# Moving the first attention pass ahead of the scan's preparation, with a new timetable for the scans

## The reference

```python
# first attention: 16 heads in 8 pairs, 4 sequences of 256 tokens, slots M=64
q, k, v, s = x@Wq, x@Wk, x@Wv, clip(x@Ws)      # per head
# slot attention in closed form: e = exp(s), z = cumsum(e) over time
ok = tril(q k^T) @ e / z ; p = softmax(ok * scale) ; o = tril((p/z) e^T) @ v
o = rmsnorm(o) * g_norm_weight * silu(x@Wg) ; x = layernorm(x + o@Wo)
# state-space block: u = silu(conv(in_proj @ ctx)); dt, B, C = x_proj @ u
delta = softplus(dt_proj @ dt + bias)           # 256 channels
for n in range(16):                             # state index
    state_n[t] = state_n[t-1] * exp(delta*A_n) + (delta*u) * B_n[t]
    y += state_n * C_n
```

## Time and profile before

| | us |
|---|---|
| time, median of 3 runs | 1022.68 (1022.05 to 1022.96) |
| profiled execution, its own time | 1022.48 |
| its span | 1020.7 |
| PE busy | 884.8 (87%) |
| DVE busy | 766.3 (75%) |
| ACT busy | 503.4 (49%) |
| POOL busy | 423.3 (41%) |

### The profile page before, as it was taken

How to read it: one execution, slowest core, us unless ns; L and a number is a source line. 1 busy time by engine, 2 the same in 40 slices (tenths; PEclk the granted TensorE clock), 3 DMA queues, 4 the chain that set the end, 5 groups by cost and what they waited for, 6 DMA issues and landing times.

```text
span 1020.7 us, 16012 instructions
## 1 busy us (share of the span) xinstructions
PE 884.8 (87%) x5239; PEld 571.3 (56%) x5239; DVE 766.3 (75%) x1372; ACT 503.4 (49%) x971; POOL 423.3 (41%) x338
## 2 busy tenths in 40 slices
PE   6789999999999999977788999899826785899886
PEld 2446565656666666655576766677614573343443
DVE  6759797878787878879783554666467688998797
ACT  3554545444444445444344433345523338898485
POOL 1244738292837464554204433243277332121013
PEclk9789999999999999997899999999957898999998
DMA  5812112112121121100805999899643100000001
GB/s 183 277 60 67 62 57 68 61 51 77 51 64 64 62 67 62 62 1 1 248 22 181 303 301 298 271 288 285 187 126 93 51 1 2 6 7 7 1 6 37
DMA packets 53840, 105.08 MB, mean 103 GB/s; under 512 B 8569, under 2 KB 26305, under 8 KB 53281
## 3 DMA queue, kind: packets, MB, share of 16 engines
q1 hardware_dynamic: 48033, 88.76, 26.7%
q0 software_dynamic: 5760, 15.74, 6.0%
HBM read 87.34 MB, written 17.14 MB: 102 GB/s over the span
## 4 chain that ended last, share of the span: by engine, by line
PE 44%; DVE 27%; DMA 9%; issue 8%; POOL 5%; ACT 5%; SPq 2%; DVEq 0%; POOLq 0%; ACTq 0%
PE ps L717 5%; PE ps L893 4%; PE ps L802 4%; DMA w_dn<-in_w_dn 4%; PE ps L682 4%; PE ps L905 3%; DVE row_max L2550 3%; POOL key_part L1453 3%; PE ps L1225 2%; PE ps L672 2%; DVE state L2009 2%; DMA key_part<-y_dram,slot_idx 2%; DMA y_dram<-y_out 2%; PE ps L730 2%; PE ps L1211 2%
## 5 line engine op out<-in xcount | busy, mean ns | idle before, releaser
L1374 POOL TENSOR_TENSOR state<-state,c_row 128x1024 f32<-128x1024 f32 x32 | 77.3, 2416 | 181.7 <-DVE state L2009 99.1
L1425 POOL DMA_INDIRECT xg<-x_dram,tok_of x68 | 65.4, 962 | 147.3 <-PE ps L951 102.1
L717 PE MATMUL ps<-w_vg,xT 128*128 128x512 f32 x256 | 118.9, 609 | 7.6 <-DVE th L2033 7.6
L893 PE MATMUL ps<-w_gv,xgT 128*128 128x352 f32 (+1 forms) x272 | 91.2, 480 | 0.5 <-DMA w_dn<-in_w_dn 0.2
L1367 POOL TENSOR_TENSOR drive<-du,b_row 128x1024 f32<-128x1024 f32 x32 | 90.3, 2823 | 0.2
L672 PE MATMUL ps<-xT,w_qks 128*128 128x512 f32 x192 | 85.0, 593 | 0.7 <-DMA w_qks<-in_wqks 0.7
L2020 DVE TENSOR_TENSOR aT<-ps,tri 128x768 f32<-128x768 f32 x64 | 60.0, 956 | 33.8 <-PE ps L682 33.3
L2009 DVE TENSOR_TENSOR_SCAN state<-decay,drive 128x1024 f32<-128x1024 f32 x32 | 83.9, 2624 | 0.0
L2550 DVE TENSOR_REDUCE row_max<-ps 128x4 f32<-128x1024 f32 x64 | 74.3, 1218 | 7.1 <-PE ps L1190 6.3
L717 PEld LDWEIGHTS ps<-w_vg,xT 128*128 128x128 f32 x256 | 47.4, 196 | 56.7 <-issue 45.6
L1377 POOL TENSOR_TENSOR y<-y,state 128x1024 f32<-128x1024 f32 x32 | 75.4, 2357 | 2.5
(11 more groups left out here) (308 smaller groups left out, 1981.2 us busy)
## 6 DMA issues: line engine op xcount, KB each, us to landing
w_gv<-in_w_gv SPq DMA_DIRECT2D x68, 352.0 KB
w_dn<-in_w_dn SPq DMA_DIRECT2D x68, 176.0 KB
y_dram<-y_out SPq DMA_DIRECT2D x68, 128.0 KB, 7.0
b_row<-x_dbl_dram SPq DMA_DIRECT2D x16, 512.0 KB, 3.5
c_row<-x_dbl_dram SPq DMA_DIRECT2D x16, 512.0 KB, 4.8
y_dram<-blank SPq DMA_DIRECT2D x4, 1408.0 KB, 13.1
w_vg<-in_wvg SPq DMA_DIRECT2D x8, 512.0 KB, 3.2
w_qks<-in_wqks SPq DMA_DIRECT2D x8, 384.0 KB, 2.9
```

What stands on the lines that cost most here:

```text
L717: last = mm(bank(PJ + t % 2), xT[:, k, t * P:(t + 1) * P], w_vg[:, k, :], start=(k == 0), stop=(k == KD - 1))
L893: last = mm(ps[:, j, 0:2 * F], x_of(k), w(k), start=(k == 0), stop=(k == KD - 1))
L1374: G.tensor_tensor(state[:, n % 2], state[:, n % 2], c_row[:, j], ALU.mult).then_inc(read_out, 1)
```

## The change

Pass 0 of the attention is placed ahead of the scan's preparation. `conv` now lies in `state`, `aux` and `aux2` in `drive` (four buffers in place of two), `x_pad` in the rows' buffers, `x_dbl` in `wT`. The projections for `x_dbl` (`inner_rows`) and for the step size (`step_size`) are PE work inside pass 0, in the banks of the scores; the softplus is spread over pass 0 on ACT and DVE. No unit of the scan runs in pass 0, five run in each of passes 1 to 6, two in the last. Two of the five follow each other behind the masks; the first stands ahead of the gates. The drives are made four units ahead. POOL reads the two units behind the masks only when both are scanned. The slot sums and their product with epsilon lie in PSUM from pass 1 on. The loops over passes are unrolled.

```diff
+SLOTS = ("front", "masks", "masks2", "gated", "clip")
+SCANS = ((),) + (SLOTS,) * 6 + (("front", "gated"),)
+        drive = sb("drive", [P, LEADS, TOK])
+        conv = state[:]
+        x_dbl = wT[0:XD]
+        aux = drive[:, 0:ET]
+        aux2 = drive[:, ET:2 * ET]
...
                 project_vg(0)
+                if i == 0:
+                    scores(0, range(2, 3))
                 project_vg(1)
+                if i == 0:
+                    scores(0, range(3, 4))
+                    inner_rows()
...
                 project_vg(2)
+                if i == 0:
+                    step_size(0)
                 project_vg(3)
...
+                    if i == 0 and t == 4:
+                        step_size(1)
...
+            def read_and_drive(i, slots):
+
+                units = [SCAN_AT[i, slot] for slot in slots if slot in SCANS[i]]
+                for m in units:
+                    read_of(m, units[-1] if "masks2" in slots else m)
+                for m in units:
+                    if m + LEADS < STATE_UNITS:
+                        drive_of(m + LEADS)
...
+            for i in range(PAIRS):
+                read_and_drive(i, ("front",))
+                read_and_drive(i, ("masks", "masks2"))
+                if i < PAIRS - 1:
+                    pool.wait_ge(zT_ready, i + 2)
+                read_and_drive(i, ("gated", "clip"))
...
+            def exp_plus_one():
+                dve.wait_ge(scan_act, 13)
+                V.tensor_scalar(aux, conv, 1.0, None, ALU.add).then_inc(softplus_step, 1)
+                dve.wait_ge(softplus_step, 1)
+                V.scalar_tensor_tensor(out=conv, in0=aux, scalar=-1.0, in1=conv, op0=ALU.add,
+                                       op1=ALU.subtract).then_inc(softplus_step, 1)
...
-                scan(i, 1)
+                if i == 0:
+                    exp_plus_one()
+                scan_at(i, "masks")
+                scan_at(i, "masks2")
...
-                V.scalar_tensor_tensor(out=ss[:], in0=ss[:], scalar=1.0 / DV, in1=eps_sq[:], op0=ALU.mult,
+                V.scalar_tensor_tensor(out=ss[:], in0=ss[:], scalar=1.0 / DV, in1=eps, op0=ALU.mult,
...
-                scan(i, 2)
+                scan_at(i, "gated")
...
                     clip_slots(i + 1)
-                    scan(i, 3)
-                    dve.wait_ge(decay_ready, at(i, 4, 4))
-                    V.tensor_copy(a_cur[:], a_neg[:, :, bass.ds(2 * i + 2, 2)]).then_inc(a_picked, 1)
+                    scan_at(i, "clip")
+                    if i == 0:
+                        add_logs(0)
                     add_mixed(0)
...
                     add_mixed(3)
-                    mask_scores(i + 1, Y)
+                    if i == 0:
+                        add_logs(1)
+                    mask_scores(i + 1)
```

More of the change, by code:

```diff
@@ L136 @@
 TURN = dict(x1=0, x2=1, att0=2, x3=3, x4=4)
+STATE_UNITS = DS * ET
+LEADS = 4
+SLOTS = ("front", "masks", "masks2", "gated", "clip")
+SCANS = ((),) + (SLOTS,) * 6 + (("front", "gated"),)
+SCAN_AT = {at_slot: n for n, at_slot in enumerate((i, slot) for i in range(PAIRS) for slot in SCANS[i])}
+assert len(SCAN_AT) == STATE_UNITS
 def at(i, per, c):
@@ L684, in both_heads, with scores, inner_rows, step_size @@
                 return last
-            def scores(i, which, odd_bank):
+            def scores(i, which):
                 pe.wait_ge(qk_copied, at(i, 4, 4))
                 for b in which:
[L690 to L693, removed]
+                    if b >= 2:
                         pe.wait_ge(scores_masked, at(i, 4, b - 1))
-                    both_heads(odd_bank if b % 2 else AB, kT, qT, b).then_inc(scores_ready, 1)
+                    both_heads(Y if b % 2 else AB, kT, qT, b).then_inc(scores_ready, 1)
+            def inner_rows():
+                pe.wait_ge(scan_consts, 96)
+                pe.wait_ge(u_ready, 2)
+                pe.wait_ge(scores_masked, 3)
+                for half in range(2):
+                    for e in range(ET):
+                        last = mm(ps[0:XD, AB + half, :], xp_w[:, e, :], u[:, e, half * 512:(half + 1) * 512],
+                                  start=(e == 0), stop=(e == ET - 1))
+                    last.then_inc(scan_mm, 1)
+            def step_size(e):
+                if e == 0:
+                    pe.wait_ge(x_dbl_copied, 2)
+                else:
+                    pe.wait_ge(scan_act, 8)
+                for half in range(2):
+                    mm(bank(AB + half), dt_w[:, e * P:(e + 1) * P], x_dbl[0:DR, half * 512:(half + 1) * 512],
+                       start=True, stop=True).then_inc(scan_mm, 1)
             def step(i, last_pair):
@@ L815, in step @@
                 if not last_pair:
-                    scores(i + 1, range(B), Y)
+                    scores(i + 1, range(B))
             pe.wait_ge(scan_consts, 48)
@@ L825, in _ @@
             project_qks(0, True, range(6))
[L826 to L832, removed]
-            pe.wait_ge(const_loaded, 48)
[L834 to L844, removed]
+            pe.wait_ge(const_loaded, 48)
+            pe.wait_ge(inner_copied, 4)
+            scores(0, range(2))
+            for i in range(PAIRS):
+                step(i, i == PAIRS - 1)
             pe.wait_ge(wkv_loaded, 16)
@@ L2035, in gate @@
                                            op1=ALU.mult).then_inc(gate_ready, 1)
+                scan_at(i, "front")
                 gate(0)
                 gate(1)
-                scan(i, 0)
+                if i == 0:
+                    all_sums()
+                sums = slot_sum[:] if i == 0 else ps[:, AB, 384:384 + 2 * TILES]
+                eps = eps_sq[:] if i == 0 else ps[:, AB, 384 + 2 * TILES:384 + 4 * TILES]
                 dve.wait_ge(slots_ready, at(i, 1, 1))
```

295 lines of the change are left out of this document (153 added, 142 removed).

## The result

The changed kernel takes 1033.82 us (median of four timings, 1032.4 to 1037.75); the kernel before took 1022.37 beside it. The ratio is 1.0124, 95% interval 1.0086 to 1.0162: slower. The prediction said 1030.0, with a range of 1016 to 1037.

What follows compares the result with a forecast made beforehand. PE, busy 87% of the span, had almost no empty time between passes 0 and 7. Steady passes +25.8, pass 0 -11.1, pass 7 -7.4 make +7.3 on 1022.48: 1029.8, told as 1030.0 us, range 1016 to 1037.

Steps and rivals of the forecast that it cites:

- The steady passes: Passes 1 to 6: the period becomes 57.6 us, 4.3 more each, 25.8 in all; bounds 0.3 to 5.5 a pass.
- three predicted waits: Tail of passes 1 to 6: scan behind on, scan behind the clip and slot sums each wait for POOL, at most 2.35.
- Pass 0: Up to the end of pass 0: pass 1 begins at 92.0 instead of 103.16, a gain of 11.1 us; bounds 8 to 14.
- The head: Pass 0 up to the reads: they begin at 52.9, the second at 53.8 instead of 70.86, 17.0 us gained.
- The 1.6 us more: Pass 0, by the skill's rule, not adopted: second gating waits for POOL's first y, u 1.6 us later, time 1031.4.
- The slot sums in a row: Doubt about the tail of pass 0: the two slot sums may go in a row, a gain of 2.3 us more.
- Pass 7: Last pass: fewer scans and no hold by POOL on ss or ln_shift save 7.4 us; bounds 5 to 8.
- Smaller waits: Rival, tails of passes 1 to 6: DVE need not wait for POOL; 1005.8 us, or about 1015 with one wait; chance 0.20.
- the deciding 56.0: Passes 1 to 6: growth of 2.75 us a pass decides; below it the change is faster.
- TensorE's clock in the new gaps: Rival, PE ahead of project_out(2) and (3): clock falls with each gap, 2.1 us a pass, time 1042.6; chance 0.06.
- the prediction's own signs of being wrong: Periods near 54 with tail scans of 2.28, PE gaps waiting for a row's load, or clock under 1.00 in passes 1 to 6.
- Pass 0 gains nothing: Rival, pass 0: preparation stretches it so that only 3 us are won, time 1038; chance 0.04.

Runs made afterwards that it cites:

- Experiment 1: Changed kernel with POOL's two drives of the pair moved behind the wait for the slot sums in five-unit passes; 1019.04 us, ratio 0.9978 to the kernel before.
- experiment 3: Changed kernel with the slot sums of squares and their product with epsilon back in SBUF in all passes; 1032.57 us, ratio 1.0102 to the kernel before.
- experiment 4: Changed kernel with five units in passes 1 to 4 and four in passes 5 to 7; 1025.59 us, ratio 1.0036 to the kernel before.
- experiment 2: Changed kernel with ACT copying the next pair's first q piece ahead of the third square; 1040.13 us, ratio 1.0155 to the kernel before.
- experiment 7: Experiment 1 with POOL's du in pass 0 also held behind the slot sums; 1038.58 us, ratio 1.0024 to the kernel before.
- experiment 5: Kernel before with its loops over the passes written out on every engine, nothing else changed; 1041.39 us, ratio 1.0061 to the kernel before.
- experiments 8 and 9: Both: Experiment 1 with the timetable of experiment 4; 8 also holds du in pass 0 (1033.38 us, ratio 0.9988), 9 does not (1014.43 us, ratio 0.9917).

## Why the prediction was right

*The steady passes.* Predicted 57.6 us each, 4.3 more than before; measured 57.8. (From its own rows the end of `add_mixed(1)` at 52.0 and the 5.7 us behind it make 57.7.) All three predicted waits are in the rows: 4.04 behind `on` (predicted "some 4.2"), 3.20 behind the clip (3.3), and 2.77 for the two slot sums. Experiment 1 takes two of the three away and the period falls to 55.4; of the remaining 2.1 above 53.3, some 1.2 is the third wait and 0.9 PE's stall for ACT's copy, by the estimate given there; in the changed kernel the longer waits hide that stall, as predicted. The six passes cost 27.3 us (347.03 less the 319.73 from 103.16 to 422.89); 25.8 was predicted. The taking of turns, read from one scan and one `ss` row, carried over to the slot sums, on which it had not been seen. The Trainium skill (SBUF — State Buffer, Who interferes with whom) says that a DVE instruction with two SBUF inputs contends with a GpSimd one that reads SBUF, and that issue order decides who blocks; the rows of `ss`, 0.17 us with one operand in PSUM and 2.34 with both in SBUF (experiment 3), agree.

*Pass 0.* Predicted 92.0, measured 95.94: the gain of 11.1 us was 7.2, under the lower bound of 8. This is the term of the sum that was mis-sized most. The head was late by 1.5 us (reads at 54.44 instead of 52.9), and 1.1 of it was there from the start: PE's first projection stands at 12.07, where the prediction took the 10.99 of the earlier trace rows. The 1.6 us more that the prediction reckoned for `u`, were the second gating to wait for POOL's whole instruction, did not come: the two operations of the second gating took 1.06 and 1.23 us beside POOL's `tensor_scalar`, against 0.68 and 1.23 for the first, and `u` was 0.8 late. Such a wait is not excluded by the rows, though: in the kernel before, the same product at 21.72 took 2.02 us, 0.8 more than the first, with POOL's `tensor_scalar` begun at 21.27. The tail cost the rest. DVE, POOL and PE of the changed kernel:

```profile
79.80 5.23 DVE L2044 TENSOR_TENSOR_SCAN zT<-ones,eT 128x256 f32<-128x256 f32 x2
...
79.43 2.36 POOL L1424 TENSOR_TENSOR du<-delta,u 128x1024 f32<-128x1024 f32 x1 [45.34 <-DVE delta L2092]
81.87 2.60 POOL L1400 TENSOR_TENSOR drive<-du,rows_bc 128x1024 f32<-128x1024 f32 x1
...
85.75 3.29 PE L849 MATMUL ps<-w_o,oT 128*128 128x256 f32 x8 [3.53 <-DVE xres L2168]
...
93.08 2.93 PE L701 MATMUL ps<-qT,kT 64*128 64x256 f32 x16 [2.22 <-DVE aT L2066]
```

`add_mixed(1)` was predicted to end at 84.3 and ended at 85.60, 1.3 late, as late as the head had made everything. So the waits for POOL's `du` and drive had the right size. `project_out(3)` behind it was predicted to end at 86.0 and ended at 89.04, 3.0 late. What was left out is the clock behind the gap of 3.53 us: its eight matmuls take 3.29 us, against 1.89 for the eight before them, and the last scores 2.93, against 1.79 in the steady passes. The windows of the two say why, granted clock 0.58 and 0.51, near 1.2 GHz:

```profile
85.70:89.00 3.30, 3.25 (x10) 2.21 (x10) 1.66 (x3) 2.11 (x2) 0.00 (x0) 0.58 0.00 0
93.00:96.00 3.00, 2.92 (x17) 2.35 (x17) 1.85 (x3) 0.00 (x0) 2.92 (x2) 0.51 0.00 0
```

That is 2.5 us together; with the 1.5 of the head it accounts for the 3.9 by which pass 1 was late. The 2.5 is not fixed: behind the same gap of 3.53 us the two rows took 3.59 and 1.79 us in experiment 4 and 2.60 and 1.79 in experiment 2. The slot sums in a row (a gain of 2.3 by the prediction's doubt) did not come. Holding `du` and its drive back (experiment 7) lets pass 1 begin 2.9 us sooner, of which 2.2 or less last past it.

*Pass 7.* Predicted 7.4 us less, measured 7.3: it begins 20.1 later than before, and the row that normalises the residual 12.7 later. `ln_shift` takes 0.17 us instead of 1.62.

*Behind the attention.* In the profiled runs the router's matmuls come 13.4 us later and the span ends 15.2 later; the medians differ by 11.5. The 4 us between this profiled execution and its median lie within what executions of one kernel show here, and no view says which part of them is whose. The written-out loops, 0.6% dearer in experiment 5 on another chip, are not needed for the loss: 13.4 of the 15.2 us stand before the router's matmuls begin, where written-out loops changed nothing.

*The rivals.* Smaller waits: refuted, the period is above the deciding 56.0 (53.3 and 2.75), with all three waits seen; experiment 1 makes this rival true for two of the three waits, and its 55.4, just under the deciding point, brings the time to about that of the kernel before. TensorE's clock in the new gaps: not at every pass as priced (2.1 us each). The granted clock is 1.00 in passes 1 and 2 and 0.97 in 3 to 6, which is one of the prediction's own signs of being wrong; but the periods lie between 57.58 and 58.00, 0.4 us apart, since the slow matmuls of `project_out(2)` (3.12 us at 375.71 in pass 5) lie beside the wait for `add_mixed(1)`. It took 2.5 us in pass 0, where no rival had placed it, and 1.3 to 2.3 a pass in experiment 2. Pass 0 gains nothing: refuted, it gained 7.2.

The sum by measured terms, in the profile: 27.3 for six passes (20.1 and 7.2), less 7.2, less 7.3, is 12.8, and the router's matmuls are at +13.4. The prediction's sum was 7.3: 3.9 of the difference is pass 0 and 1.5 the steady passes. So the waits that decide the sign were foreseen, and the time fell inside the range although pass 0 lay outside its own bounds.

## What to carry to other kernels

When two engines take turns at their operands, as DVE and POOL do here, count in every pass not only how long each is busy but which of the other's instructions will stand beside the last links of the chain; an instruction that costs nothing under cover can cost its whole length there. Moving two POOL instructions a few us later was worth twice as much (14.4 us) as the rearranged first pass (7.2), and giving the last passes four units in place of five and two took the ratio on from 0.9978 to 0.9917 (on two chips; by the router's row 3.3 us). A wait of TensorE that is removed ahead of a bound elsewhere only lengthened the next gap, from 2.13 to 3.13 us, and where the clock fell behind that gap the pass became 1.3 to 2.3 us longer. And an earlier start is no gain by itself: of the 1.9 us between the starts of pass 1 in experiments 8 and 9, 0.45 was left one pass later.

## What the runs showed of the hardware that was not expected

The granted clock of one and the same program differs by place and execution, behind gaps of the same length too (experiment 2, and pass 0 above). In the kernel before, the transposes ahead of the router took 2.50 us behind a gap of 2.24 in one profile and 3.17 behind 3.32 in another, and the router's 32 matmuls 3.68 and 4.32; in two other kernels 6.93, one of them the kernel before with its loops written out. Timeline of PE in the second profile of the kernel before:

```profile
493.76 3.17 PE L863 MATMUL ps<-ident,xres 128*128 128x128 f32 x16 [3.32 <-DVE xres L2174]
496.72 4.32 PE L886 MATMUL ps<-w_router,xT 128*128 128x64 f32 x32
```

One and the same kernel, the one before, took 1036.0 us on one chip (29 timings) and 1021.2 on another (11). The attention is not where they differ: with its loops written out it had the same periods on both. Most of the distance arises at two places behind it: the first rows of `w_dn`, in the experts, stand at 554.03 on the first chip and 557.32 on the second, the turn of `k_st` behind the experts at 744.18 and 735.57, and the matmuls on `lqT` of the linear attention at 824.51 and 802.99. From there on the distance stays between 21.5 and 22.9, as the first rows of `row_max` show. What causes it is open, with one execution on each:

```profile
875.26 1.23 DVE L2550 TENSOR_REDUCE row_max<-ps 128x4 f32<-128x1024 f32 x1 [2.99 <-PE ps L1190]
```

```profile
853.73 11.57 DVE L2550 TENSOR_REDUCE row_max<-ps 128x4 f32<-128x1024 f32 x10 [2.99 <-PE ps L1190]
```
